# Gated tiles five and six ahead of the roundings, with keys, roots and zeros rearranged, and value products in the second and fourth head of a quad

## The reference

```python
x = x + _L0_xattn_ref(_layernorm(x), ctx, ...)      # banded attention-free mixing, then a two-layer net
x = x + _L0_ffn_ref(_layernorm(x), w_gate, w_up, w_down)
x = x + _L1_xattn_ref(_layernorm(x), ctx, ctx, mask, Wq, bq, Wk, bk, Wv, bv, Wo, bo)   # 16 heads of 8
x = x + _L1_ffn_ref(_layernorm(x), ...)              # 8 experts, the best one of each token
```

```python
def _act_quant(x):
    scale = 127.0 / jnp.clip(jnp.max(jnp.abs(x), axis=-1, keepdims=True), 1e-05)
    return jnp.clip(jnp.round(x * scale), -128.0, 127.0) / scale
gate = silu(_bitlinear(x, w_gate)); up = _bitlinear(x, w_up)
return _bitlinear(gate * up, w_down)                 # _bitlinear rounds its input by rows
```

## Time and profile before

| | before |
|---|---|
| median of 3 runs | 245.91 us |
| lowest and highest | 245.41 and 246.24 us |
| the profiled execution | 246.41 us |
| its span (first to last record) | 244.6 us |
| granted TensorE clock, mean of the span | 0.965 |
| PE, DVE, ACT, POOL busy | 79%, 72%, 55%, 46% of the span |

### The profile page before, as it was taken

How to read it: one execution, slowest core, us unless ns; L and a number is a source line. 1 busy time by engine, 2 the same in 40 slices (tenths; PEclk the granted TensorE clock), 3 DMA queues, 4 the chain that set the end, 5 groups by cost and what they waited for, 6 DMA issues and landing times.

```text
span 244.6 us, 4754 instructions
## 1 busy us (share of the span) xinstructions
PE 192.2 (79%) x1750; PEld 135.3 (55%) x1750; DVE 175.4 (72%) x455; ACT 135.1 (55%) x271; POOL 112.5 (46%) x205
## 2 busy tenths in 40 slices
PE   0378865998565768688989979978878896999994
PEld 0268654887332556553333534534546784798883
DVE  4678889899887779778757776886665555749252
ACT  2136755929894558336677667767793347260200
POOL 8131677985496076811787784774030032000000
PEclk9999999999996879997999999999999997999999
DMA  6994040000000000000000000000000000000000
GB/s 177 353 390 203 0 162 15 0 3 0 1 3 0 0 0 3 3 3 3 0 1 4 0 3 1 0 3 0 3 1 3 0 1 3 0 3 21 24 21 21
DMA packets 4461, 8.75 MB, mean 36 GB/s; under 512 B 514, under 2 KB 3026, under 8 KB 4052
## 3 DMA queue, kind: packets, MB, share of 16 engines
q1 hardware_dynamic: 3636, 7.78, 8.7%
q10 hardware_dynamic: 800, 0.63, 0.9%
HBM read 7.89 MB, written 0.52 MB: 34 GB/s over the span
## 4 chain that ended last, share of the span: by engine, by line
PE 32%; DVE 26%; POOL 19%; issue 10%; ACT 9%; DMA 2%; SPq 1%; POOLq 0%; DVEq 0%
PE ps L1364 27%; POOL gate_pt L541 6%; PE ps L1373 4%; POOL w L431 3%; DVE mx L1202 3%; POOL rstd L410 3%; DMA wf<-weights_dram 2%; DVE stats L851 2%; DVE hid_xm L1010 2%; DVE half_c L1192 2%; DVE amax L1085 1%; ACT gate_pt L811 1%; DVE gate_pt L1079 1%; DVE ka_mem L1051 1%; POOL spread L528 1%
## 5 line engine op out<-in xcount | busy, mean ns | idle before, releaser
L1202 DVE TENSOR_REDUCE mx<-ps 128x2 f32<-128x512 f32 x64 | 42.3, 686 | 16.5 <-PE ps L1364 16.4
L811 ACT ACTIVATE gate_pt<-ps 128x512 f32<-128x512 f32 x64 | 37.1, 602 | 15.8 <-PE ps L1364 15.3
L1364 PE MATMUL ps<-w,hid_xm 128*128 128x256 f16 (+1 forms) x288 | 30.3, 263 | 0.5 <-DVE hid_xm L1010 0.5
L541 POOL TENSOR_SCALAR gate_pt<-ka_mem 32x256 f16<-32x256 f16 x64 | 25.6, 401 | 4.4 <-issue 0.2
L1364 PE MATMUL ps<-gate_pt,half_c 128*128 128x512 f16 x64 | 25.0, 393 | 3.2 <-issue 1.8
L1364 PEld LDWEIGHTS ps<-w,hid_xm 128*128 128x128 f16 x288 | 25.4, 101 | 3.7 <-POOL w L423 0.7
L1364 PE MATMUL ps<-qb,gate_pt 128*128 128x256 f16 x128 | 25.5, 282 | 0.8
L1364 PE MATMUL ps<-gate_pt,hid_xm 128*32 128x256 f32 x256 | 20.4, 390 | 1.5 <-ACT gate_pt L811 1.5
L1364 PEld LDWEIGHTS ps<-qb,gate_pt 128*128 128x128 f16 x128 | 9.5, 100 | 18.7 <-issue 11.0
L528 POOL TENSOR_SCALAR spread<-mx 128x16 f16<-128x16 f32 x32 | 5.9, 204 | 24.6 <-DVE mx L1202 18.4
L410 POOL TENSOR_TENSOR rstd<-vareps,halfs 128x2 f32<-128x2 f32 (+1 forms) x19 | 15.9, 838 | 1.6
(11 more groups left out here) (222 smaller groups left out, 503.9 us busy)
## 6 DMA issues: line engine op xcount, KB each, us to landing
stage<-weights_dram SPq DMA_DIRECT2D x2, 1024.0 KB, 11.3
wf<-weights_dram SPq DMA_DIRECT2D x4, 256.0 KB, 8.5
wf<-mask_dram SPq DMA_DIRECT2D x1, 1024.0 KB, 4.8
eb_oT<-ffw_dram SPq DMA_DIRECT2D x1, 768.0 KB, 8.3
ctx_in<-ctx_rows_dram ACTq DMA_DIRECT2D x4, 128.0 KB, 5.5
x_in<-x_dram SPq DMA_DIRECT2D x4, 128.0 KB, 3.1
gate_pt<-ctx_cols_dram SPq DMA_DIRECT2D x1, 512.0 KB, 8.5
out_dram<-ctx_in SPq DMA_DIRECT2D x4, 128.0 KB, 1.7
```

Source lines behind the costliest of these rows:

```text
L541: ins = nc.gpsimd.tensor_scalar(kz[part, n % KRING, k], ka[part, b, quad], 1.0, 0.0, ALU.mult, ALU.add)
L811: nc_act(pt[:, head % PRING].rearrange("p t n -> p (t n)"), ps[:, 2 + head % 2, :], ACT.Exp, scale=DK ** -0.5).then_inc(sig["probs"], 1)
L1202: V.tensor_reduce(mx[:, b, head:head + 2, t], score_bank(4 * n + i).rearrange("p (h n) -> p h n", h=2), AX.X, ALU.max).then_inc(sig["smax" ...
L1364: return nc.tensor.matmul(dst, lhsT, rhs, start=start, stop=stop, skip_group_check=True)
```

## The change

ScalarE takes the silu of the third pair's tiles, 4 and 5, before it rounds the first two sequences, and 6 and 7 behind that rounding and ahead of the first column copies. PE makes the products of tiles 6 and 7 before it turns the first two sequences. Behind `down`, the key products, the turning of the query rows and their copies are interleaved: `keys(0, 1)` goes ahead of `down(3)`, the rows of sequences 0 and 1 are turned ahead of `keys(1..3, 1)`, and the read of the flag moves behind the turning. VectorE takes the sequences in pairs, with statistics, roots and rows of 0 and 1 ahead of the sums of 2 and 3, and makes the flag behind the first statistics. The roots of this norm are taken by pairs (two powers of 4 columns in place of four of 2), GpSimd's zeroing of `spread` and `va` moves between earlier roots, and that of `kz` between the two pairs' roots. `split_hi("m2")` moves behind the key copies. In the loop the value products follow the scores of k = 1 and k = 3. The work is the same otherwise.

```diff
-         (LN_ATT, (0,)), (LN_ATT, (1,)), (LN_ATT, (2,)), (LN_ATT, (3,)),
+         (LN_ATT, (0, 1)), (LN_ATT, (2, 3)),
...
 GpSimd:
-            for first in range(0, B, 2):
-                rstd_of(LN_OUT, first, first + 1)
-                rstd_of(LN_FFN, first, first + 1)
-
-            pool.wait_ge(sig["gscale"], 1)
+            rstd_of(LN_OUT, 0, 1)
             nc.gpsimd.memset(spread[:, :, :, :], 0.0)
+            rstd_of(LN_FFN, 0, 1)
+            rstd_of(LN_OUT, 2, 3)
             pool.wait_ge(sig["ff_mm"], B)
             nc.gpsimd.memset(va[:, :, :, :, DK:32], 0.0).then_inc(sig["zeros_ready"], 1)
             pool.wait_ge(sig["zeros_ready"], 1)
             nc.gpsimd.memset(va[:, :, :, :, DK:DK + 1], 1.0).then_inc(sig["zeros_ready"], 1)
+            rstd_of(LN_FFN, 2, 3)
...
-            pool.wait_ge(sig["kscale"], 2)
+            rstd_of(LN_ATT, 0, 1)
+            pool.wait_ge(sig["g"], len(GU_ORDER))
             nc.gpsimd.memset(kz[:, :, :, :], 0.0).then_inc(sig["zeros_ready"], 1)
-            for b in range(B):
-                rstd_of(LN_ATT, b)
+            rstd_of(LN_ATT, 2, 3)
...
 ScalarE:
+            gate(4)
+            gate(5)
             round_gated(0)
             round_gated(1)
-            gate(4)
-            gate(5)
+            gate(6)
+            gate(7)
             gated_columns(0)
-            gate(6)
             gated_columns(1)
-            gate(7)
             round_gated(2)
             round_gated(3)
             gated_columns(2)
             gated_columns(3)
+            key_hi(0, 1)
+            act.wait_ge(sig["resmask"], 2)
+            query_columns(0)
+            query_columns(1)
+            for b in range(1, B):
+                key_hi(b, 1)
             split_hi("m2")
-            for b in range(B):
-                key_hi(b, 1)
-            act.wait_ge(sig["resmask"], 2)
-            for b in range(B):
-                act.wait_ge(sig["turned"], nth(T_QUERY, b))
-                nc_act(colsA[:, 0, b], bank(b, 0)[:, 0:T], ACT.Copy).then_inc(sig["cols_hi"], 1)
+            query_columns(2)
+            query_columns(3)
...
 VectorE, behind down_scales(2) (the old loop, L1157 to L1189, is taken out):
+            ffn_residual(0)
+            ffn_residual(1)
+            att_stats(0)
+            flags()
+            att_rows(0)
+            att_rows(1)
+            ffn_residual(2)
+            ffn_residual(3)
+            att_stats(2)
+            key_lo(0, 1)
+            query_columns_lo(0)
+            query_columns_lo(1)
+            key_lo(1, 1)
+            att_rows(2)
+            att_rows(3)
+            key_lo(2, 1)
+            key_lo(3, 1)
+            query_columns_lo(2)
+            query_columns_lo(3)
...
 TensorE (query_turned(b) is the old wait for the rows and the turning, L1604 to L1607):
             gate_up(4)
             gate_up(5)
+            gate_up(6)
+            gate_up(7)
             gated_turned(0)
             gated_turned(1)
-            gate_up(6)
-            gate_up(7)
             down(0)
             down(1)
             gated_turned(2)
             gated_turned(3)
             down(2)
+            keys(0, 1)
             down(3)
-
-            for b in range(B):
+            query_turned(0)
+            query_turned(1)
+            for b in range(1, B):
                 keys(b, 1)
+            query_turned(2)
+            query_turned(3)
             pe.wait_ge(sig["flag_ready"], 3)
             general = pe.value_load(flag_i[0:1, 0:1], min_val=0, max_val=B * T * T)
...
-                        if k < TILES and n >= 1:
-                            weighted_values(n - 1, k)
+                        if k % 2 == 1 and n >= 1:
+                            weighted_values(n - 1, k // 2)
```

More of the change, by code:

```diff
@@ L735, in gated_columns, with query_columns @@
                        bias=-MAGIC).then_inc(sig["q2T_ready"], 1)
+            def query_columns(b):
+                act.wait_ge(sig["turned"], nth(T_QUERY, b))
+                nc_act(colsA[:, 0, b], bank(b, 0)[:, 0:T], ACT.Copy).then_inc(sig["cols_hi"], 1)
+            gate(4)
+            gate(5)
             round_gated(0)
             round_gated(1)
-            gate(4)
-            gate(5)
+            gate(6)
+            gate(7)
             gated_columns(0)
-            gate(6)
             gated_columns(1)
-            gate(7)
             round_gated(2)
@@ L1156, in _, with flags, ffn_residual @@
             down_scales(2)
[L1157 to L1163, removed]
-            for b in range(B):
+            def flags():
+                dve.wait_ge(sig["colmask"], 1)
+                V.tensor_tensor(flag_f[:, 0:2], mask_sums[0:1, 0:2], mask_sums[0:1, 2:4], ALU.add).then_inc(sig["flag_ready"], 1)
+                dve.wait_ge(sig["flag_ready"], 1)
+                V.scalar_tensor_tensor(flag_f[:, 2:3], flag_f[:, 0:1], -T / (4 * BIG), flag_f[:, 1:2], ALU.mult, ALU.add)\
+                    .then_inc(sig["flag_ready"], 1)
+                dve.wait_ge(sig["flag_ready"], 2)
+                V.tensor_copy(flag_i[:, :], flag_f[:, 2:3]).then_inc(sig["flag_ready"], 1)
+            def ffn_residual(b):
                 dve.wait_ge(sig["down_mm"], b + 1)
@@ L1171, in _, with att_stats, att_rows, query_columns_lo @@
                 ins.then_inc(sig["x2"], 1)
[L1172 to L1181, removed]
-                ln_rows(LN_ATT, b, lambda t: x2[:, b, t])
[L1183 to L1187, removed]
+            def att_stats(first):
+                for b in (first, first + 1):
+                    dve.wait_ge(sig["x2"], b + 1)
+                    ln_stats(LN_ATT, b, lambda t: x2[:, b, t])
+                for b in (first, first + 1):
+                    ln_moments(LN_ATT, b)
+            def att_rows(b):
+                ln_rows(LN_ATT, b, lambda t: x2[:, b, t])
+            def query_columns_lo(b):
                 dve.wait_ge(sig["cols_hi"], nth(C_QUERY, b))
                 lo_part(colsA[:, 1, b], bank(b, 0)[:, 0:T], colsA[:, 0, b], "cols_ready")
+            ffn_residual(0)
[17 more added lines that the diff above has]
+            query_columns_lo(3)
             def query_lo(b):
@@ L1584, in down, with query_turned @@
                 ins.then_inc(sig["down_mm"], 1)
+            def query_turned(b):
+                pe.wait_ge(sig["rows_ready"], nth(R_ATT, b))
+                for t in range(TILES):
+                    ins = transposed(bank(b, 0)[:, t * P:(t + 1) * P], rows[:, b, t])
+                ins.then_inc(sig["turned"], 1)
             gate_up(4)
             gate_up(5)
+            gate_up(6)
+            gate_up(7)
             gated_turned(0)
             gated_turned(1)
-            gate_up(6)
-            gate_up(7)
             down(0)
```

## The result

The changed kernel takes 245.14 us (median of 20 runs, 243.01 to 246.59); the kernel before, run beside it, 247.01 (20 runs). The ratio is 0.9917, 95% interval 0.9894 to 0.9941: 0.83% faster, some 2.05 us, where 4.2 us (1.7%) was forecast. 245.14 also lies above the range of 239.9 to 244.6.

What follows compares the result with a forecast made beforehand. No engine was the bound by itself: engines hand over and wait between gated layer and queries, and PE waits in the loop. From 245.91 us, -2.2 and -2.0 gave -4.2, so 241.7, range 239.9 to 244.6.

Steps and rivals of the forecast that it cites:

- the cover of the `kz` zeroing: Ahead of the queries: zeroing of 3.51 us hidden while VectorE sums and takes second statistics; at most 3.5 if uncovered.
- it stands until 92.1 and not 88.65: Rival, ahead of the queries: VectorE's first row scaling cannot run beside the `kz` zeroing; 3.45 late, 245.2 us, chance 0.10.
- the pair at 4.48: Kernel start: scaling pair from SBUF took a plain 0.48 us despite a zeroing, cited against the zeroing holding scalings.
- Part one: Gated layer to queries: reordering forecast to gain 2.2 us, bounds 0 and 2.8.
- The order of the silus: Gated layer: silus first gain VectorE 1.22 us; last maximum and factor come about 2.5 earlier, at 84.4.
- The zeroing of `va`: Between earlier roots: goes into waits of GpSimd, counted as nothing, bounded by the `kz` zeroing's cost.
- VectorE's list: Last factor to last row scaling: VectorE's own work sets the end, at 95.4, 2.8 us earlier.
- Part two: Attention loop: moved value products cover a 0.49 us wait at quad boundaries; forecast gain 2.0 us, bounds 0 and 3.2.
- The sums do not come late: Rival, gated layer: copies behind the later turning hold VectorE by all the silus gave; 243.9 us, chance 0.05.
- GpSimd does not pace the loop: Rival, loop: GpSimd's 3.5 us a quad and the chain through the rows decide everywhere; 243.7 us, chance 0.20.
- `out_copy`: Rival, end of even quads: ScalarE's copies wait for later value products; seven cost 5.5 us, 249.2 us, chance 0.07.
- The clock did fall: Rival, ahead of the queries: PE's short turnings let its clock fall; costs 1.3 us, 243.0 us, chance 0.18.

Runs made afterwards that it cites:

- `kz_mid`: Changed kernel with `kz` in its own memory, zeroed by GpSimd behind the residual masks; ratio 0.9825 to the kernel before (-4.3 us).
- `va_back`: Changed kernel with the zeroing of `va` back behind the feed-forward root of the last two tiles; queries 45.84 us behind the statistics, no ratio given.
- `stage_only`: Changed kernel with the loop's value products back at a quad's first and second head; ratio 1.0052 to the kernel before.
- `stage_kz_mid`: `kz_mid` with the value products back at a quad's first and second head; ratio 0.9939 to the kernel before (-1.5 us).
- `kz_early`: Changed kernel with `kz` in its own memory, zeroed by GpSimd at the kernel's start; ratio 0.9833 to the kernel before (-4.1 us).
- `rows_one_op`: Changed kernel with the multiply by the root left out of the row scalings ahead of the queries; four took 3.96 us, no ratio given.

## Why the prediction was wrong, step by step

**The step that failed** is the cover of the `kz` zeroing: "runs from 88.6 to 92.1 while VectorE sums and takes the second statistics". Directly ahead of those sums stand the first pair's scalings, and they wait for the same root as the zeroing does. The prediction had this as a rival, "it stands until 92.1 and not 88.65", with a price of 3.45 and a time of 245.2; measured were 245.14, and a price of 2.8 to the queries (46.48 against 43.65 in `kz_mid`), 2.97 of it in the scalings (4.08 against 1.11); in the whole time it is 2.3 (-2.05 against -4.3). The sign that it named, a scaling of over 1 us beside the zeroing, is there with 3.51. The price was somewhat too high; the chance of 0.10 was the mistake. That the rival's time comes within 0.1 of the measured one is luck: it counts from 245.91, the median of three runs, and the twenty runs beside the changed kernel have 247.01. By that base the forecast would have been 242.8; of the 3.4 us between 241.7 and 245.14, 1.1 are the base and 2.3 the zeroing.

The chance came from one row, the pair at 4.48 "although a zeroing ran from 3.78 to 4.73". They overlapped for only 0.25 us, which is less than one scaling takes, so the row could not tell a held one from a free one. That was to be seen in the row.

The Trainium skill, "SBUF — State Buffer", section "Who interferes with whom", says that a copy, a cast or this kind of scaling can be shut out for a whole GpSimd instruction, while one with two SBUF inputs contends only with GpSimd work that reads SBUF and a reduction never does. The runs here agree: 4.08 and 1.14 for four scalings of the two forms and 0.67 for a maximum, beside a zeroing.

**Part one without it.** The order of the silus did its work, with a smaller size. The queries were forecast 2.24 sooner (96.4 for 98.64); `kz_mid` has 1.43. Of the 0.8 that is missing, 0.45 is there by the last factors: they release GpSimd's rounding at 86.72 in `kz_mid`, which is 84.85 by the time of before, and 84.4 was forecast. The zeroing of `va`, which was to "go into waits of GpSimd", holds VectorE's clamp there (0.54 of ScalarE's wait, 0.64 at the queries by `va_back`). VectorE's list from the factors on is 0.24 longer than summed: its wait for the first root is 1.03 and not 0.4, because the flag's three instructions, which were to cover 0.9 of it, take only 0.5. The flag read is 0.53 to 0.62 and not 0.3. The second turning under 2 us and its full clock were right, and so was a pair slowed beside the copies (1.60 for four in place of 1.11).

**Part two** was right in mechanism and small in size: 2.7 us (78.9 to 76.2) for 2.0. Its bound of 3.2 is a wrong sum, twice 1.4 and 0.2 make 3.0; the gain is inside both. By GpSimd's shift rows, in kernels without a low clock there (`stage_only` against `va_back`), three quads of the first period get shorter by 0.26, 0.35 and 0.25, for which 1.0 was taken, and one of the second by 0.24. The quad with the tail step, of which I said the covered gap "only makes that wait longer", gets 0.67 shorter, twice. The first quads keep their length, as said.

TensorE at that tail step, before (the wait of 1.24 is the row at 146.94) and after:

```profile
147.31 0.64 PE L1364 MATMUL ps<-gate_pt,hid_xm 128*32 128x256 f32 x8
```

```profile
144.79 0.64 PE L1387 MATMUL ps<-gate_pt,hid_xm 128*32 128x256 f32 x8
...
147.47 0.44 PE L1396 MATMUL ps<-cst,rows 128*128 128x128 f32 x2 [1.50 <-ACT rows L646]
147.75 0.38 PE L1387 MATMUL ps<-qb,gate_pt 128*128 128x256 f16 x2
```

The wait does get longer, 1.50 for 1.24. But a value product of 0.57 that stood behind it now runs ahead of it, and the scores follow the turning at once. The sum had left that out.

**The rivals.** The sums do not come late: VectorE waits 0.21 us for TensorE there in the changed kernel and 0.25 in `kz_mid`, where up to 0.2 was summed. GpSimd does not pace the loop at the old length. `out_copy` (L769 after) waits 0.9 us in four times, not 5.5. The clock did fall: in the changed kernel from 95.8 to 99.2, under the keys, ahead of rows that were late anyway. In `kz_mid` it comes behind TensorE's waits of 1.59, 0.49 and 0.62 us ahead of the queries, and lies on them (0.50 is 1.2 of 2.4 GHz):

```profile
101.00:103.00 2.00, 2.00 (x11) 1.44 (x10) 0.00 (x0) 0.92 (x1) 1.72 (x5) 0.50 0.04 8
```

There queries to first scores take 6.16 us, against 5.46 before and 5.50 in `stage_kz_mid`, where the clock stayed full: 0.7, not 1.3. So a clock that falls there costs something, though not in the changed kernel. What makes it fall is not shown: `stage_kz_mid` has nearly the same waits (1.59, 0.49 and 0.53).

**The sum.** Part one -1.4 and the loop -2.7 make -4.1 without the zeroing, and `kz_mid` measured -4.3. That this is so near the forecast's -4.2 is luck: part one was taken 0.8 too large and the loop 0.7 too small. With the zeroing in its place, part one is +1.06 to the first scores (51.60 for 50.54), as the shorter way from the queries to them gives 0.3 back; +1.06 - 2.7 = -1.6, inside the changed kernel's interval of -2.6 to -1.5. Run singly, the two parts gave +1.3 and -2.5.

## What to carry to other kernels

Before GpSimd work is moved "into a wait", list what VectorE issues while it runs, and of which form: operations of one tensor in SBUF (scalings, casts, clamps) were held beside it here, those of two tensors and reductions went on beside a zeroing. Two pieces of work that wait for the same event start together, so one isn't cover for the other. And a row is evidence against contention only if the overlap is longer than the instruction: look at the longest single instruction, not at a merged pair.

## What the runs showed of the hardware

A held VectorE instruction ends with the zeroing, whenever it started: two casts that start 0.14 us apart in `kz_early` both end at 10.4, and a scaling's 0.33 us became 3.51, ending some 0.08 us behind the zeroing (92.23 + 3.51 = 95.74, and 92.31 + 3.51 = 95.82 in `rows_one_op`). Eight short zeroings without a pause hold it like one long one (3.785 us beside 3.79).

The operation of two tensors isn't always free. `nmr` takes 1.23 us in the changed kernel, where it stands beside GpSimd's scaling of the mask (L483, 68.17 to 70.07) and ends with it, and 0.16 in `va_back`, where it stands beside a zeroing. GpSimd reads SBUF in the one and only writes in the other; that it is the reading was not tried by itself.
The same section of the Trainium skill ("SBUF — State Buffer", "Who interferes with whom") has this case too, as contention with a GpSimd instruction that reads SBUF.
